# Keys and queries stored once as halves and read back by two transfers each, in a four-layer gated cross-attention kernel

## What is computed

```python
# x (4, 256, 256); context (4, 512, 256); 16 heads of 16 columns
x = x + tanh(g_xattn[0]) * xattn0(layernorm(x), context, mask)   # scores clipped to 50, layernorm behind it
x = x + tanh(g_ffn[0])   * moe0(layernorm(x))                    # 8 experts, 2 chosen, and a shared one
x = x + tanh(g_xattn[1]) * memory1(layernorm(x), context, mask)  # one head, context as keys and values
x = x + tanh(g_ffn[1])   * moe1(layernorm(x))
x = x + tanh(g_xattn[2]) * xattn2(layernorm(x), context)         # rounded to int8 steps around it
x = x + tanh(g_ffn[2])   * signs2(layernorm(x))                  # weights are signs, relu
x = x + tanh(g_xattn[3]) * xattn3(layernorm(x), context)         # rms-normed q and k, two softmaxes (257 and 255 keys)
x = x + tanh(g_ffn[3])   * moe3(layernorm(x))                    # 16 experts, 6 chosen
```

## Time and profile before

| | us |
|---|---|
| median of three runs | 1186.84 (1183.28 to 1188.63) |
| profiled execution, its time | 1182.87 |
| its span, first to last instruction | 1181.0 |
| TensorE busy | 1021.6 |
| VectorE busy | 800.9 |
| ScalarE busy | 570.5 |
| GpSimd busy | 380.6 |

### The profile page before, as it was taken

The page is one execution under the profiler, slowest core; times in us unless marked ns, Lnnn a source line. Parts: engine busy times, 40 slices in busy tenths (PEclk is TensorE's granted clock), DMA queues, the critical chain, the costliest instruction groups (busy, mean ns, idle before and its releaser), DMA issues.

```text
span 1181.0 us, 19127 instructions
## 1 busy us (share of the span) xinstructions
PE 1021.6 (87%) x6456; PEld 767.5 (65%) x6456; DVE 800.9 (68%) x1639; ACT 570.5 (48%) x1129; POOL 380.6 (32%) x423
## 2 busy tenths in 40 slices
PE   4799878999888897779999876699999989999998
PEld 3566546877766686655665565365655578887887
DVE  6477759567866367578887675677766365676676
ACT  2677753444433343316567543146555545444443
POOL 5312214355303245331211231422110043554553
PEclk8999989999988899879999998699999999999999
DMA  6957523554320277685640254927240144555544
GB/s 201 260 134 171 124 71 103 168 156 126 116 90 4 80 140 189 168 155 136 140 98 21 68 107 134 193 54 172 86 92 4 30 132 123 157 153 159 147 151 129
DMA packets 87050, 145.85 MB, mean 124 GB/s; under 512 B 10413, under 2 KB 42438, under 8 KB 84538
## 3 DMA queue, kind: packets, MB, share of 16 engines
q1 hardware_dynamic: 77562, 111.36, 31.6%
q0 software_dynamic: 9408, 33.45, 15.9%
HBM read 113.41 MB, written 32.41 MB: 123 GB/s over the span
## 4 chain that ended last, share of the span: by engine, by line
PE 54%; DVE 16%; DMA 9%; issue 7%; ACT 6%; POOL 5%; SPq 2%; DVEq 0%; ACTq 0%; POOLq 0%
PE psum L617 33%; PE psum L910 6%; PE psum L877 5%; PE psum L886 5%; DMA ff_raw<-in_ff 5%; ACT probs L1059 2%; DMA weights_out<-combine 2%; DVE nmx L1371 1%; POOL ff_wl L1955 1%; DVE nmx L1368 1%; DVE nmx L1369 1%; DVE ff_s L1994 1%; PE psum L836 1%; POOL keys L1122 1%; DMA keys<-keys_out 1%
## 5 line engine op out<-in xcount | busy, mean ns | idle before, releaser
L617 PE MATMUL psum<-ff_xh,ff_wh 128*128 128x512 f32 x424 | 177.7, 419 | 33.9 <-POOL ff_wl L1955 29.9
L2011 DVE TENSOR_TENSOR ff_hl<-ff_h,ff_hh 128x512 fp32r<-128x512 f32 x114 | 121.8, 1069 | 98.4 <-ACT ff_hh L1896 97.8
L1061 ACT ACTIVATE probs<-psum 128x512 f32<-128x512 f32 x256 | 144.6, 597 | 86.1 <-PE psum L877 82.3
L1955 POOL TENSOR_TENSOR ff_wl<-ff_raw,ff_wh 128x512 fp32r<-128x512 f32 x92 | 120.5, 1310 | 173.2 <-ACT ff_wh L1907 173.1
L877 PE MATMUL psum<-queries,keys 128*128 128x512 f32 x384 | 153.4, 429 | 12.2 <-ACT probs L1059 7.4
L617 PE MATMUL psum<-ff_xh,ff_wl 128*128 128x512 f32 x392 | 157.1, 401 | 0.0
L1907 ACT ACTIVATE ff_wh<-ff_raw 128x512 fp32r<-128x512 f32 x92 | 58.0, 630 | 183.1 <-DMA ff_raw<-in_ff 181.0
L617 PE MATMUL psum<-ff_wh,ff_hh 128*128 128x256 f32 x456 | 131.5, 292 | 10.3 <-DVE ff_hl L2011 10.3
L886 PE MATMUL psum<-keys,queries 128*128 128x512 f32 x256 | 119.6, 484 | 15.6 <-DVE nmx L1369 8.9
L617 PE MATMUL psum<-ff_wh,ff_hl 128*128 128x256 f32 x456 | 130.5, 290 | 0.0
L617 PEld LDWEIGHTS psum<-ff_xh,ff_wh 128*128 128x128 f32 x424 | 83.3, 196 | 58.0 <-POOL ff_wl L1955 35.9
(11 more groups left out here) (263 smaller groups left out, 2154.8 us busy)
## 6 DMA issues: line engine op xcount, KB each, us to landing
ff_w<-weights_out SPq DMA_DIRECT2D x94, 256.0 KB
ff_raw<-in_ff SPq DMA_DIRECT2D x92, 256.0 KB, 3.6
keys_out<-keys_turned SPq DMA_DIRECT2D x36, 512.0 KB, 4.4
keys<-keys_out POOLq DMA_DIRECT2D x48, 384.0 KB, 7.5
ff_raw<-in_ff SPq DMA_DIRECT2D x106, 128.0 KB, 2.1
queries_out<-queries_turned SPq DMA_DIRECT2D x36, 256.0 KB, 3.2
queries<-queries_out POOLq DMA_DIRECT2D x32, 256.0 KB, 4.3
w_raw<-in_w SPq DMA_DIRECT2D x12, 256.0 KB, 3.7
```

The source lines that it names most:

```text
L617: last = eng.matmul(dst, lhs[i](k), rhs[j](k), start=start and n == 0, stop=stop and n == groups * len(pairs) - 1, skip_group_check=True)
L1061: ins = eng.activation(dst, src, ACT.Exp, scale=SCALE)
L1955: then(eng.tensor_tensor(ff_wl[:, slot, 0:2 * D], raw(n, slot)[:, 0:2 * D], ff_wh[:, slot, 0:2 * D].bitcast(F32), ALU.subtract), "f_w1r")
L2011: then(eng.tensor_tensor(ff_hl[:, slot, :], ff_h[:, slot, :], ff_hh[:, slot, :].bitcast(F32), ALU.subtract), "f_hr")
```

## The change

Keys are written as two groups of rows (lo, hi) and queries as two (hi, lo); the place that a third copy took in memory is gone. A read of keys is now two transfers, one of both groups (32 rows) and one of the high group again (16 rows); a read of queries is one of the high group (16 rows) and one of both and, in blocks 2 and 3, the constants (48 rows; 32 in block 0). So 24 writes go (12 of 512 KB and 12 of 256 KB), and 96 read transfers become 192 with the same bytes. What the partitions hold afterwards is the same. The tables of places are set anew.

```diff
-    kd = nc.dram_tensor("keys_out", (B, 2, 3, HD, NP, M), F32, kind="Internal").ap()
-    qd = nc.dram_tensor("queries_out", (B, 2, 4, HD, NP, S), F32, kind="Internal").ap()
+    kd = nc.dram_tensor("keys_out", (B, 2, 2, HD, NP, M), F32, kind="Internal").ap()
+    qd = nc.dram_tensor("queries_out", (B, 2, 3, HD, NP, S), F32, kind="Internal").ap()
...
-        return 16 * 4 * (B // 2 * (0, 2, 3).index(blk) + b // 2 + 1)
+        return 16 * 8 * (B // 2 * (0, 2, 3).index(blk) + b // 2 + 1)
...
-            return 16 * 3 * (B * layer + b + 1)
+            return 16 * KC * (B * layer + b + 1)
...
                 for m in range(2):
-                    src = kd[b, m, :, :, pairs, :].rearrange("s r j c -> (s r) j c")
-                    move(kst[buf(b)][64 * m:64 * m + AUG, pairs, :], src, f"d_r{buf(b)}{ph}")
+
+                    src, r = kd[b, m, :, :, pairs, :].rearrange("s r j c -> (s r) j c"), 64 * m
+                    move(kst[buf(b)][r:r + 2 * HD, pairs, :], src, f"d_r{buf(b)}{ph}")
+                    move(kst[buf(b)][r + 2 * HD:r + AUG, pairs, :], src[HD:2 * HD], f"d_r{buf(b)}{ph}")
...
-                slots = 4 if peak else 3
+                slots = 3 if peak else 2
                 for m in range(2):
-                    src = qd[b, m, 0:slots, :, pairs, :].rearrange("s r j c -> (s r) j c")
-                    move(qst[buf(b)][64 * m:64 * m + HD * slots, m, pairs, :], src, f"d_r{buf(b)}{ph}")
+
+                    src, r = qd[b, m, 0:slots, :, pairs, :].rearrange("s r j c -> (s r) j c"), 64 * m
+                    move(qst[buf(b)][r:r + HD, m, pairs, :], src[0:HD], f"d_r{buf(b)}{ph}")
+                    move(qst[buf(b)][r + HD:r + HD * (slots + 1), m, pairs, :], src, f"d_r{buf(b)}{ph}")
...
-                for slot, half in enumerate((1, 0, 1)):
+                for slot, half in enumerate((0, 1)):
...
-                for slot, half in enumerate((0, 0, 1)):
+                for slot, half in enumerate((0, 1)):
...
-        ("qr", 1, -8.8), ("v", 0, -16), ("ve", 0, -14.5), ("v", 1, -12.2), ("ve", 1, -7.7)],
+        ("qr", 1, -8.8), ("v", 0, -16), ("ve", 0, -15.7), ("v", 1, -11.6), ("ve", 1, -7.7)],
...
-        ("qr", 0, -8.8), ("kr", 1, -0.5), ("qr", 1, -8.3), ("v", 0, 5.2), ("ve", 0, 5.8), ("v", 1, 8.2),
+        ("qr", 0, -4.8), ("kr", 1, 5.9), ("qr", 1, -1.9), ("v", 0, 7.6), ("ve", 0, 8.2), ("v", 1, 10.6),
...
-FIRST_SHIFT = {0: -16.4, 2: -14, 3: -6.6}
+FIRST_SHIFT = {0: -16.4, 2: -14, 3: 0.8}
```

More of the change, by code:

```diff
@@ L101 @@
         3: ("ot", "oe", "wo", "wd")}
-HOOKS = [{0: [("late", "ot"), ("late", "oe")], 1: [("late", "wo")], 2: [("late", "wd"), ("late", "wr")],
-         3: [("late", "wn")], 4: [("statistics", 1)], 5: [("normal", 1)],
-         6: [("turn", 1), ("halves", 1)], 7: [("logits", 1)], 8: [("route", 1, 0)],
-         9: [("route", 1, 1)], 10: [("route", 1, 2)], 11: [("weights", 1)], 12: [("combine", 1)],
-         15: [("add", 0)], 16: [("mem", "scale"), ("extra", 0), ("extra", 1)],
-         17: [("mem", "round")], 18: [("mem", "diag")], 19: [("mem", "whole")],
-         20: [("mem", "spread")], 21: [("mem", "normal")], 22: [("mem", "turn")],
-         23: [("mem", "context0")], 24: [("mem", "context1")], 25: [("mem", "mask")],
-         26: [("mem", "kept")]},
+HOOKS = [{0: [("late", "ot"), ("late", "oe")], 1: [("late", "wo")], 3: [("late", "wd"), ("late", "wr")],
+         4: [("late", "wn")], 5: [("statistics", 1), ("normal", 1)],
+         6: [("turn", 1), ("halves", 1)], 8: [("logits", 1), ("route", 1, 0), ("route", 1, 1)],
+         10: [("route", 1, 2)], 11: [("weights", 1)], 12: [("combine", 1)], 15: [("add", 0)],
+         16: [("mem", "scale"), ("extra", 0), ("extra", 1)], 17: [("mem", "round")],
+         18: [("mem", "diag"), ("mem", "whole")], 19: [("mem", "spread")], 20: [("mem", "normal")],
+         21: [("mem", "turn")], 22: [("mem", "context0")], 23: [("mem", "context1")],
+         24: [("mem", "mask")], 25: [("mem", "kept")]},
          {-1: [("logits", 0), ("route", 0, 0), ("route", 0, 1), ("route", 0, 2)],
-         0: [("weights", 0), ("combine", 0)], 1: [("statistics", 1)],
-         2: [("normal", 1), ("turn", 1)], 3: [("halves", 1), ("logits", 1)], 4: [("route", 1, 0)],
-         5: [("route", 1, 1)], 6: [("route", 1, 2)], 7: [("weights", 1)], 8: [("combine", 1)],
+         0: [("weights", 0), ("combine", 0), ("statistics", 1)], 1: [("normal", 1)],
+         2: [("turn", 1), ("halves", 1)], 3: [("logits", 1)], 4: [("route", 1, 0)],
+         5: [("route", 1, 1)], 6: [("route", 1, 2)], 7: [("weights", 1)], 9: [("combine", 1)],
          11: [("add", 0)]},
-         {0: [("late", "ot"), ("late", "oe")], 1: [("late", "wo")], 2: [("late", "wd")],
+         {0: [("late", "ot")], 1: [("late", "oe")], 2: [("late", "wo"), ("late", "wd")],
          3: [("late", "wn")], 4: [("statistics", 1)], 5: [("normal", 1), ("extra", 0)],
@@ L122 @@
          {0: [("late", "ot"), ("late", "oe")], 1: [("late", "wo")], 2: [("late", "wd")],
-         3: [("statistics", 1)], 4: [("normal", 1)], 5: [("turn", 1)], 6: [("halves", 1)],
-         7: [("logits", 1)], 8: [("route", 1, 0)], 9: [("route", 1, 1)], 10: [("route", 1, 2)],
-         11: [("weights", 1)], 12: [("combine", 1)], 26: [("add", 0)]}]
+         3: [("statistics", 1), ("normal", 1)], 4: [("turn", 1)], 5: [("halves", 1)],
+         6: [("logits", 1)], 7: [("route", 1, 0)], 8: [("route", 1, 1)], 9: [("route", 1, 2)],
+         10: [("weights", 1)], 12: [("combine", 1)], 26: [("add", 0)]}]
 LEADS = {2: {9: [("au", 0), ("kt", 0, 0), ("kt", 0, 1), ("ke", 0, 0), ("ke", 0, 1), ("kw", 0)],
@@ L190 @@
 SUM_AFTER = {0: 5.6, 2: 7.8, 3: 4.6}
-FOLLOW = {0: (17.6, 4.6, 18.8), 2: (26.2, 9.2, 0), 3: (25.6, 9.2, 23.2)}
+FOLLOW = {0: (17.6, 4.6, 20), 2: (30.2, 9.2, 0), 3: (25.6, 9.2, 25.6)}
 CHAINS = {
@@ L225, in check_order @@
     assert asked == taken, blk
-MISC = {"au": -20, "ng": 0.3, "nt": 1.8, "ne": 2.3, "nw": 2.4, "nr": 2.5, "cl": 1.4, "ev": 0.3, "fx": 3.5, "fw": 3, "fv": 32, "fe": 1.2, "lg": 4, "ro1": 1.5, "ro2": 3.5, "ct": 6, "ce": 6.8}
+MISC = {"au": -20, "ng": 0.9, "nt": 2.1, "ne": 2.3, "nw": 2.4, "nr": 2.5, "cl": 1.4, "ev": 0.3, "fx": 3.5, "fw": 3, "fv": 32, "fe": 1.2, "lg": 4.6, "ro1": 1.5, "ro2": 3.5, "ct": 6, "ce": 6.8}
 def order(blk):
@@ L2465, in rows_of_queries @@
                 src = a["aug_q"].rearrange("r (one c) -> r one c", one=1)
-                load(qd[b, :, 3].rearrange("m r j c -> r m (j c)"), src.to_broadcast([HD, 2, NP * S]), "d_aq")
+                load(qd[b, :, 2].rearrange("m r j c -> r m (j c)"), src.to_broadcast([HD, 2, NP * S]), "d_aq")
         load(gate_raw[:, :, :], a["gate0"], "d_gate")
```

## The result

| | before | changed |
|---|---|---|
| median of 4 runs each, us | 1185.07 (1183.28 to 1188.63) | 1152.82 (1150.08 to 1155.20) |
| profiled execution, its time | 1182.87 | 1155.20 |
| its span | 1181.0 | 1153.3 |

(The kernel before has one run more here than in the table ahead of the prediction.) The changed kernel was measured twice more, beside experiments: 0.9743 (0.9705 to 0.9782) and 0.9762 (0.9732 to 0.9791).

What follows compares the result with a forecast made beforehand. TensorE's work (busy 1021.6 of 1181.0 us) plus its standstills bound the kernel. Terms -1.7 + 1.5 - 0.5 - 1 - 7 + 0.6 = -8.1 us gave 1174.8 for the profiled execution, 1178.8 as median; range 1167 to 1191.

Steps and rivals of the forecast that it cites:

- The hooks of the MoE layers: MoE layers: hooks move by a place or two between tiles; priced at nothing, give or take a microsecond.
- Layer 3's start: Start of layer 3's attention: reads issued ahead of batch 1's root remove waits; -7 us (-10 to 0), first read +0.6.
- if the zeroing now holds up VectorE in front of a chain of its own: Layer 3: listed among the signs that would show the prediction wrong; no size given.
- Traffic: Keys and queries through memory: 31.7 us of DMA time freed by fewer writes, 38 us spent on split reads.
- Prologue: Before the first score: saved writes shorten the chain, split reads cost a little; -1.7 us (-2.7 to +1).
- End of layer 0's attention: GpSimd's six more read issues delay the root and what follows it; +1.5 us (0.3 to 2.5).
- ff1's middle: Layer 2's keys amid ff1's weight loads: one write less, two keys pairs in pieces; -0.5 us (-1.8 to +1.3).
- Layer 2: Layer 2's attention: first maxima go out sooner with queries' second half asked for apart; -1 us (-2 to +1).
- more: Rival: TensorE stays busy through layer 3's start and its clock with it; 1171 down to 1167 us, chance 0.12.

Runs made afterwards that it cites:

- y4: Kernel before with only the hooks of all four MoE layers set as in the changed kernel; ratio 0.9900, -12 us.
- x3: Kernel before with only ff1's hooks set anew (statistics and normalisation one tile earlier, combine one later); ratio 0.9912, -10 us.
- w4: Changed kernel with ff1's hooks put back as before; ratio 0.9841 against the kernel before, -19 us.
- z1: Kernel before with the new tables and reads split in two, but three writes as before; ratio 0.9821, -21 us.
- v1: Kernel before with the new tables, old movement, and the zeroing of queries put behind four constants reads in layers 2 and 3; ratio 0.9805, -23 us.
- x1: Kernel before with the new movement alone (two writes, split reads), all tables old; ratio 0.9982, -2 us.
- w3: Second measurement of x1, the new movement alone on the kernel before; ratio 0.9990, -1 us.
- y1: Changed kernel measured again, against the kernel before; -30 us.
- y2: Kernel before with all new tables, but three writes and unsplit reads as before; ratio 0.9834, -20 us.
- w1: Kernel before with the new movement and only layer 3's new tables; ratio 0.9870, -15 us.
- w2: Kernel before with the new movement and the new hooks of all MoE layers; ratio 0.9883, -14 us.

## Why the prediction was wrong

**The step that failed** is the one on what is not layer 3: "The hooks of the MoE layers move by a place or two between tiles: nothing, give or take a microsecond." They are worth 12 us (y4), 10 of them in ff1 (x3, and w4 in reverse), half of the 24 us by which the forecast missed. The rows that show it were in the trace of before: a wait of 3.80 us on ff_xn and one of 2.04 behind it. The prediction read the stretches in which keys and queries move and gave the hooks no term and no reason for it; it never asked what stands ahead of a moved instruction in VectorE's queue.

**Layer 3's start** was right in mechanism and near in size. The stretch was forecast at 30 us from 37.5 and is 28.9. Its parts were not as told. The tables alone give 6 (31.8); what the movement adds, 3.5, is mostly the zeroing that no longer falls on xn (2.4 with the reads split alone, z1, and 2.7 in v1). The prediction has no term for it and names it only as a sign of being wrong, "if the zeroing now holds up VectorE in front of a chain of its own". It had held VectorE up before, for 1.7 us at `rms`; the new tables alone move this to xn, and a microsecond of issues keeps it clear. That the split reads would do so was not foreseen, so this part of the near size is luck. With it in, the two parts work together for 5 us, which a sum of separate terms can't hold.

**Traffic.** The balance of 31.7 us freed against 38 spent was wrong on the second number: the queue's busy time rose by 9 us, so the pieces of 16 and 32 rows don't go as slowly as the 117 and 165 GB/s that the prediction took from its nearest rows. About zero is what the movement gives alone all the same (x1, w3), but not for that reason: layer 3's old order gave some of it back (39.3 for 37.5). Under the new order the two writes are worth 7 us, give or take 5 (z1 against the changed kernel).

**Prologue,** -1.7 forecast. TensorE is done at 38.7 as told (38.6), and then waits 2.17 us for keys:

```profile
38.40 0.28 PE L717 MATMUL psum<-bias,half_rows 128*128 128x256 f32 x1
40.85 0.50 PE L876 MATMUL psum<-queries,keys 128*128 128x512 f32 x1 [2.17 <-DMA keys<-keys_out]
```

The first score is at 41.45 before and at 40.85 now, but the profile before had an early one. Over seven traces with the old movement it starts at 41.5 to 44.4, mean 42.9, over twelve with the new at 39.0 to 42.1, mean 40.8: -2.1. (z1, with the reads split and three writes, has it at 41.8.)

**End of layer 0's attention,** +1.5 forecast, does not show: the root starts 2.1 us earlier than before, as all around it.

```profile
116.77 4.58 POOL L1121 DMA_DIRECT2D keys<-keys_out  x8
121.36 1.94 POOL L1609 TENSOR_TENSOR rstd<-ve,half_neg 128x4 f32<-128x4 f32 x1
```

It is directly behind the keys reads, with no idle time, as forecast. But the variances come at 121.25, so it is 0.1 us late and not 1.2: the reads began without the 0.45 us wait that they had, and the twelve issues took 6.6 us (114.73 to 121.35) against 4.2 for six (117.35 to 121.53), 2.4 more instead of 3.1.

**ff1's middle,** -0.5 forecast. The load of 11.67 us is one of 9.11 now, and TensorE's wait behind it is 2.05 us where it was 7.13 (first the row of before, then two of now):

```profile
481.12 0.80 PE L617 MATMUL psum<-ff_xh,ff_wh 128*128 128x512 f32 x1 [7.13 <-POOL ff_wl L1955]
```

```profile
454.03 9.11 DMA ff_raw<-in_ff
```

```profile
465.18 0.50 PE L616 MATMUL psum<-ff_xh,ff_wh 128*128 128x512 f32 x1 [2.05 <-POOL ff_wl L1958]
```

From 460 to 505 the changed kernel gains 4.2 us and y1 3.4, the tables alone 2.0 (y2), the movement alone 1.1 and 1.9 (x1, w3). Over all traces it is 1.1 to 4.2, mean 2.7, with the new movement (twelve) and up to 2.8, mean 1.2, with the old (seven). So 1 to 2 us come of the movement, in the direction told and larger. **Layer 2,** -1 forecast, gave nothing: 22.8 us ahead at 505, 22.5 at 600.

**The sum.** Hooks -12, layer 3's tables -7, the movement -1.5, -5 from the last two together in layer 3: -25.5, against a mean of -30.5 for three measurements, whose intervals reach from -25 to -37. From w1 and w2, less the movement that both hold, it is -15 - 14 + 1.5 = -27.5. What stays open is whether the last 3 to 5 us are more than the spread of the totals. Of the rivals "more" came nearest in size, for another reason; TensorE's clock in the stretch went only from 0.68 to 0.71.

## What to carry to other kernels

Ask of every moved instruction what stands ahead of it on its engine, and what that waits for: an elementwise sum that waits for a transfer holds all that is queued behind it, and putting the normalisation ahead of it, one tile up in a table, gave 8 us in its stretch, where all the traffic saved gave 1 to 2 by itself. When a change has parts, measure them apart and together; here two parts worth 7 and 1.5 us were worth 15. Where totals spread by 1%, compare a short stretch between two fixed instructions in many traces: it told the four cases of layer 3 apart, and it finds a loss of 3.6 us in ff3 that no total shows.
